# A four-stage sequence model on one core: the scan's output sum split over three engines, its start rewritten, and the last two stages reordered

## The reference

```
x = _layernorm(x + _L0_attn_ref(x, ...))   # state-space scan, 64 heads of 8, state 64
x = _layernorm(x + _L0_ffn_ref(x, ...))    # 8 experts, top 2, plus a shared expert
x = _layernorm(x + _L1_attn_ref(x, ...))   # A = sum over tokens of cos_sim(K) * V;  Y = (A * rope(Q)) @ W_out
x = _layernorm(x + _L1_ffn_ref(x, ...))    # silu(x Wg) * (x Wu) @ Wd, integer weights with scales
```

```
h = a_t * h + u_t * b_t          # b_t and c_t are rotated by phi
y = einsum('bhpn,bhn->bhp', h, c_t)
```

## Time and profile before

| | |
|---|---|
| median of 3 runs | 2555.78 us (2555.35 to 2564.16) |
| the profiled execution's own time | 2558.58 us |
| its span, first to last instruction | 2556.9 us |
| mean granted TensorE clock, share of full speed | 0.928 |
| busy over the span | DVE 1908.7 us (75%), PE 2052.8 (80%), ACT 1529.7 (60%), POOL 1479.2 (58%) |
| the scan, first DVE product to last y | 202.6 to 1414.0 us |
| key-value stage | about 2044 to 2262 us |
| last stage | about 2266 to 2557 us |

### The profile page before, as it was taken

How to read it: one execution, slowest core, us unless ns; L and a number is a source line. 1 busy time by engine, 2 the same in 40 slices (tenths; PEclk the granted TensorE clock), 3 DMA queues, 4 the chain that set the end, 5 groups by cost and what they waited for, 6 DMA issues and landing times. The chain is left out here.

```text
span 2556.9 us, 60194 instructions
## 1 busy us (share of the span) xinstructions
PE 2052.8 (80%) x19761; PEld 1532.8 (60%) x19761; DVE 1908.7 (75%) x4991; ACT 1529.7 (60%) x2922; POOL 1479.2 (58%) x2287
## 2 busy tenths in 40 slices
PE   8955778878878888877887799686799857768887
PEld 5634555655556556555555688564455445558887
DVE  4547999999999999999999344466333267757776
ACT  5648999999999999999995122354122112222222
POOL 2447888888888888888887132343111154425454
PEclk9977999999999999999997899887899978989998
DMA  5766766676676776767664477343222244311110
GB/s 168 244 199 176 182 180 184 175 191 172 173 188 174 178 190 174 185 179 182 181 177 115 139 231 220 121 143 111 83 85 85 63 127 126 123 55 38 49 49 29
DMA packets 295156, 373.66 MB, mean 146 GB/s; under 512 B 44628, under 2 KB 234646, under 8 KB 294902
## 3 DMA queue, kind: packets, MB, share of 16 engines
q1 hardware_dynamic: 285030, 343.10, 48.5%
q0 software_dynamic: 9872, 27.28, 3.3%
HBM read 151.03 MB, written 85.00 MB: 92 GB/s over the span
## 5 line engine op out<-in xcount | busy, mean ns | idle before, releaser
L668 POOL TENSOR_TENSOR p_CR<-p_pc 128x256 f32<-128x256 f32 x512 | 373.8, 730 | 132.5 <-DVE p_pc L993 113.6
L749 PE MATMUL p_ps_sc<-p_CR,p_BR 64*128 64x128 f32 x4096 | 316.3, 296 | 159.4 <-DVE p_M L1010 115.5
L749 PEld LDWEIGHTS p_ps_sc<-p_CR,p_BR 64*128 64x128 f32 x4096 | 270.2, 198 | 216.9 <-issue 170.3
L672 POOL TENSOR_TENSOR p_BR<-p_pb 128x256 f32<-128x256 f32 x512 | 373.6, 730 | 36.6 <-DVE p_pb L1002 13.4
L883 ACT ACTIVATE p_D<-p_ps_x 128x512 f32<-128x512 f32 x512 | 289.7, 593 | 85.9 <-PE p_ps_x L715 84.7
L1010 DVE TENSOR_TENSOR p_M<-p_ps_sc,p_D 128x1024 f32<-128x1024 f32 x256 | 310.4, 1212 | 6.0 <-issue 3.2
L993 DVE SCALAR_TENSOR_TENSOR p_pc<-p_ps_c,p_beta,p_cs 128x256 f32<-128x256 f32 x512 | 242.9, 474 | 32.2 <-DMA p_sn<-p_tr_s 28.7
L764 PE MATMUL p_ps_y<-p_M,p_uexp 128*32 128x128 f32 x4096 | 254.0, 278 | 0.0
L1002 DVE SCALAR_TENSOR_TENSOR p_pb<-p_ps_b,p_beta,p_sn 128x256 f32<-128x256 f32 x512 | 242.6, 474 | 0.0
L1002 DVE SCALAR_TENSOR_TENSOR p_pb<-p_ps_b,p_beta,p_cs 128x256 f32<-128x256 f32 x512 | 242.5, 474 | 0.0
L993 DVE SCALAR_TENSOR_TENSOR p_pc<-p_ps_c,p_beta,p_sn 128x256 f32<-128x256 f32 x512 | 242.5, 474 | 0.0
(11 more groups left out here) (279 smaller groups left out, 5191.4 us busy)
## 6 DMA issues: line engine op xcount, KB each, us to landing
p_cs<-p_tr_c SPq DMA_DIRECT2D x256, 256.0 KB
p_sn<-p_tr_s SPq DMA_DIRECT2D x256, 256.0 KB
p_phib<-scratch_phi SPq DMA_DIRECT2D x256, 128.0 KB
p_x<-scratch_rt SPq DMA_DIRECT2D x72, 128.0 KB, 2.0
scratch_ro<-p_o POOLq DMA_DIRECT2D x72, 128.0 KB, 2.0
p_xT<-in_xT SPq DMA_DIRECT2D x64, 128.0 KB, 4.5
scratch_u<-p_u SPq DMA_DIRECT2D x16, 512.0 KB, 3.5
scratch_wu<-p_wu SPq DMA_DIRECT2D x16, 512.0 KB, 4.3
```

What stands on the lines that cost most here:

```text
L668: e.tensor_tensor(CR[:, p, g, :], pc[:, g % 2, 0, :], pc[:, g % 2, 1, :], ALU.add).then_inc(S["rotC"], 1)
L672: e.tensor_tensor(BR[:, p, g, :], pb[:, g % 2, 0, :], pb[:, g % 2, 1, :], ALU.add).then_inc(S["rotB"], 1)
L749: m = e.matmul(sc_ps[half][:, (g * 2 + b) * L:(g * 2 + b + 1) * L], BR[half * 64:half * 64 + 64, p, 2 * q + g, b * L:(b + 1) * L], CR[half ...
```

## The change

**Scan, body.** DVE's two instructions of `outputs` become one: it only scales the state's part, into the second half of a tile y of twice the size. ACT copies the chunk's part from PSUM into the first half (`sums_out`, after decays 4 and 5 of the next step). POOL adds the halves at the end of the step (`outputs`, after its last pair of rotations). ACT's second rounding pass now takes two parts u at once, 128x512 instead of twice 128x256, after every second u; so POOL's `turns` waits for a pair of parts.

**Scan, start.** The frequencies and the first angles are loaded ahead of the constants; ACT runs one Sin at once (tile warm); the sine half of the first spreading is issued by ACT's own queue; POOL no longer does `turns(2, 0, 0)` ahead of the first step; ACT's work for steps 2 and 3 is woven into step 0 (`first_step`).

**Key-value stage.** Of the four gathers of a step on POOL two move to the step's start and two stay between the two norms.

**Last stage.** `project` moves from the step's middle to the end of the step before; `turn` moves ahead of up part 2; `attention` is cut in two (sums and statistics ahead of gated part 0, the output `residual` behind it), and so is the last norm; `high_x` moves ahead of gated part 2; POOL's and ACT's streams follow.

The core of the diff in the scan (POOL's turns and its new `outputs`, ACT's new `sums_out` and its rounding, DVE's `outputs`):

```diff
             def turns(s, p, u):
...
-                at_least(e, S["mg_ok"], s, 3 * NQ, 3 * u + 3)
+                at_least(e, S["mg_ok"], s, TURNS, 5 * (u // 2) + 5)
...
+            def outputs(t, p):
+                at_least(e, S["y_ev"], t, 1, 1)
+                at_least(e, S["yx_ok"], t, 1, 1)
+                e.tensor_tensor(y[:, p, 0, :], y[:, p, 0, :], y[:, p, 1, :], ALU.add).then_inc(S["y_ok"], 1)
...
+            def sums_out(t, p):
+
+                at_least(e, S["yi_mm"], t, U, U)
+                at_least(e, S["yx_mm"], t, U, U)
+                if t >= 2:
+                    at_least(e, y_out[p], t - p, 8, 0)
+                at_least(e, S["yx_ok"], t, 1, 1)
+                e.activation(y[:, p, 0, :], yi_ps, ACT.Copy).then_inc(S["y_ev"], 1)
...
-                at_least(e, S["mg_ok"], s, 3 * NQ, 3 * u + 2)
-                e.activation(mg[:, u, :], mg[:, u, :], ACT.Copy, bias=-MAGIC).then_inc(S["mg_ok"], 1)
+                if u % 2:
+                    at_least(e, S["mg_ok"], s, TURNS, 5 * (u // 2) + 4)
+                    e.activation(mg[:, u - 1:u + 1, :], mg[:, u - 1:u + 1, :], ACT.Copy, bias=-MAGIC).then_inc(S["mg_ok"], 1)
...
-                e.tensor_tensor(yx[:, p, :], yx_ps, et[:, p, :], ALU.mult).then_inc(S["yx_ok"], 1)
-                at_least(e, S["yx_ok"], t, 1, 1)
...
-                e.tensor_tensor(y[:, p, :], yi_ps, yx[:, p, :], ALU.add).then_inc(S["y_ok"], 1)
+                e.tensor_tensor(y[:, p, 1, :], yx_ps, et[:, p, :], ALU.mult).then_inc(S["yx_ok"], 1)
```

and in the last stage, PE's step (TensorE's order; `left` counts the steps that follow):

```diff
                 up(t, p, 0)
                 if later:
                     down(t - 1, 2)
-                if not last:
-                    project(t + 1, 1 - p)
                 up(t, p, 1)
                 if later:
                     down(t - 1, 3)
+                if left:
+                    turn(t + 1, 1 - p)
                 up(t, p, 2)
-                if not last:
-                    turn(t + 1, 1 - p)
                 up(t, p, 3)
                 down(t, 0)
                 down(t, 1)
+                if left == 2:
+                    project(t + 2, p)
```

More of the change, by code:

```diff
@@ L673, in step @@
                     if g % 2:
-                        if g < NG - 1 and t + 2 < T:
+                        if t == 0:
+                            for u in ((), (0, 1), (2, 3), ())[g // 2]:
+                                turns(2, 0, u)
+                        elif g < NG - 1 and t + 2 < T:
                             turns(t + 2, p, g // 2 + 1)
@@ L679, in step @@
                             stage_u(t, p, g // 2, b)
+                    if g == 7 and t:
+                        outputs(t - 1, 1 - p)
             for s in range(2):
@@ L838, in _ @@
         def _(e):
-            e.wait_ge(S["zeroed"], 5)
-            e.wait_ge(S["const_in"], 112)
+            e.wait_ge(S["zeroed"], 1)
+            e.activation(warm[:, :], quart[:, :], ACT.Sin).then_inc(S["warm"], 1)
+            e.wait_ge(S["freq_in"], 16)
             def signed_bc(c):
@@ L946, in state, with first_step @@
                                  ).then_inc(S["x_ok" if h else "kept"], 1)
+            def first_step():
+                for n in range(2, U):
+                    decays(0, n)
+                    s, u = (2, n - 2) if n < 6 else (3, n - 6)
+                    in_turns(s, s, u)
+                    whole_turns(s, s, u)
+                turned(0, 0)
+                magnitude(2, 0)
+                for n in range(2):
+                    decays(1, n)
+                in_turns(3, 3, 2)
+                whole_turns(3, 3, 2)
+                sines(2, 0)
+                turned(0, 1)
+                in_turns(3, 3, 3)
+                whole_turns(3, 3, 3)
             def all_turns(s):
@@ L2093, in step @@
             def step(t, p):
+                if t + 2 < NC:
+                    gather(t + 2, p, 0)
                 if t:
@@ L2102, in _ @@
             for t in range(2):
-                gather(t, t)
+                for b in range(BATCH):
+                    gather(t, t, b)
             norm_pool(e, S2, N2, 0, mhalf)
@@ L2444, in down, with step @@
                 m.then_inc(S["o_mm"], 1)
-            def step(t, p, last=False):
+            def step(t, p, left=2):
                 later = not (isinstance(t, int) and t == 0)
@@ L2492, in step @@
                                      scale=gs[:, 2 * n + i:2 * n + i + 1]).then_inc(S["silu_ok"], 1)
-                    if n == 2 and not last:
+                    if n == 1 and not last:
                         copy_turned(t + 1)
@@ L2564, in sums, with last_out @@
                 e.tensor_tensor(xs[:, :, :], xm[:, :, :], xk[:, p, :, :], ALU.add).then_inc(S["xs_ok"], 1)
[L2566 to L2572 removed]
+            def last_out(t, p):
+                if not (isinstance(t, int) and t < 2):
+                    at_least(e, S["stored"][p], t - p, 8, 0)
+                norm_out(e, S2, N2, t, xs, x4[:, p, :, :])
             def step(t, p, last=False):
                 later = not (isinstance(t, int) and t == 0)
+                if not last:
+                    attention(t + 1, 1 - p)
                 gated(t, 0)
                 if not last:
[L2578 removed]
+                    residual(t + 1, 1 - p)
                 gated(t, 1)
@@ L2581, in step @@
                     sums(t - 1, 1 - p)
-                gated(t, 2)
                 if not last:
                     high_x(t + 1, 1 - p)
+                gated(t, 2)
+                if later:
+                    at_least(e, S["xs_ok"], t - 1, 1, 1)
+                    norm_stats(e, S2, N2, t - 1, xs)
                 gated(t, 3)
                 if later:
-                    last_norm(t - 1, 1 - p)
+                    last_out(t - 1, 1 - p)
             attention(0, 0)
+            residual(0, 0)
             high_x(0, 0)
```

112 lines of the change are left out of this document (61 added, 51 removed).

## The result

The changed kernel takes 2494.87 us (median of 4 runs, 2490.43 to 2499.15) against 2558.83 (4 runs, 2555.35 to 2564.16): a ratio of 0.9748, 95% interval 0.9721 to 0.9775. It is faster, but by 64 us where 98 were forecast, and lies above the forecast's range (to 2472) and above the range for 8 in 10 (to 2490). The profiled execution took 2490.43 with a span of 2488.8, 68.1 less than before.

| stretch | forecast | measured | from |
|---|---|---|---|
| scan, start to the first y product | -8.5 | -2.7 | 237.1 to 234.4 |
| scan, body | -28.4 + 3 | -15.0 | 63 steps of 18.67, now of 18.43 |
| scan, tail | +0.4 | +0.8 | last product's start to last y's end, 0.9 to 1.75 |
| key-value stage | -25 | -26.5 | first sums to PE's first Y, 216.9 to 190.4 |
| last stage | -40 + 1 | -25.0 | first Y to the end, 286.45 to 261.4 |

What follows compares the result with a forecast made beforehand. It took DVE to bound the scan and PE the last stage. Terms -8.5 - 28.4 + 0.4 + 3 - 25 - 40 + 1 = -97.5 took the profiled 2558.58 to 2461.1, median 2458 us, range 2444 to 2472.

Steps and rivals of the forecast that it cites:

- Last stage, -40: Last stage: 15 steps fall from 16.8 to 14.1 us, saving 40 us, with bounds 25 (15.1 a step) and 46.
- DVE only 0.1 below: Last stage: a walk with old durations had PE bound the step at 13.65 us, DVE finishing just under that.
- DVE bounds the last stage: Rival, last stage: waits and register instructions make DVE's step 15.1 us or more, not 14.1; about 2475 us; chance 0.08.
- The rival of the loop's jump: Last stage: jumps back, six times a pass, show on PE, costing up to 24 us, about 2475 us; chance 0.15.
- POOL's add blocks DVE: Rival, scan: each POOL add of 0.73 us holds DVE up, so 46 us come back, 2504 us; chance 0.05.
- Scan, body, -28.4: Scan body: DVE's pair of instructions becomes one, saving 0.45 us in each of 63 steps, if DVE stays the bound.
- +3 for the waits: Scan body: DVE's 7 us of waiting for the spread sines grows by 3 us, bounds 0 and 7.
- covered: Scan body: ACT's 17.5 to 17.7 us fits the new 18.22 us step; otherwise each 0.1 us more costs 6 us.
- the scan keeps its step: Rival, scan: ACT or the ring of its copies and PE's exponents needs 18.6 us; 28 us stay, 2486 us; chance 0.08.
- Scan, start, -8.5: Scan start: earlier angles and Sin table save 4.6 us, an earlier first M 4.0; together 8.5, bounds 4.6 and 11.
- the second part comes back as a later wait: Scan start: bound case where the 4.0 us from the earlier first M is lost again, leaving 4.6 us saved.
- Key-value stage, -25: Key-value stage: two fewer gathers ahead of POOL's root cut DVE's waits, saving 25 us, bounds 15 and 28.

Runs made afterwards that it cites:

- Experiment 2: Changed kernel with DVE's norm outputs in the last stage moved ahead of the roundings that start POOL's subtractions: 2464.55 us, ratio to before 0.9621.
- experiment 3: Changed kernel, order untouched, with POOL's low-part subtractions in the last stage's loop cut to 32 of 512 columns: 2467.52 us, ratio to before 0.9604.
- Experiment 4: Changed kernel with SyncE's six loads of B and C split, three in each of two scan steps: 2480.16 us, ratio to before 0.9673.
- experiments 5 and 6: Kernel before with the scan's output sum alone split over DVE, ACT and POOL: 2583.86 us; the second adds the wide rounding pass: 2547.51 us.
- experiments 8 and 9: Changed kernel with ScalarE's turns ahead of its exponentials in the first scan step: 2490.04 us; changed kernel with SyncE issuing the first sine spreading: 2489.54 us.
- experiment 11: Changed kernel with norm outputs and sum xs ahead of the roundings, B and C loads in halves, ScalarE's turns first: 2450.56 us, ratio to before 0.9538.

## Why the prediction was wrong where it was

**Last stage, -40 with "DVE only 0.1 below" PE.** The step that failed is "DVE, each piece as long as in the step of the earlier trace rows, where they make 12.33". Its pieces are not of one length wherever they stand. Before the change the norm outputs ran behind a wait for POOL's root, and so while POOL had nothing else; the new order hides that wait by putting them behind the rounding that releases POOL's subtraction. Experiment 2 moved them out, experiment 3 shortened POOL's work, and both brought 0.41 to 0.45 us and PE-bound steps back. The rival "DVE bounds the last stage" (0.08) named the right bound and nearly the right step (15.1 or more; 15.5 measured), but its cause, waits and register instructions, was wrong: it needed 2.8 us of idle on DVE a step, and there are 15.54 - 14.70 = 0.84. That the stage gained just the 25 of the forecast's near bound is luck: the bound was set for that other cause. The rival of the loop's jump is refuted by experiment 2, in which PE runs through the jumps without a gap.

The same prediction set a rule on this very port beside the rival "POOL's add blocks DVE", and there it held: DVE's products, with one input in PSUM, are still 0.47 us beside POOL's adds. I asked of the engine that *gained* work, and not of the instructions whose *neighbours* changed. The Trainium skill (SBUF — State Buffer, Who interferes with whom) has a tensor_scalar between SBUF tensors contend with GpSimd when it can run in a mode that uses both of VectorE's ports, and has the one that comes second blocked for the whole instruction of the first. The trace agrees: 0.41 us free, 1.39 at the most beside a subtraction of 1.3 to 1.4. By the same rule xs, with two SBUF inputs, should be blocked too, and it is: 1.23 against 0.69.

**Scan, body, -28.4 "if DVE stays the bound", +3 for the waits.** The saving on DVE was right, the term for the waits mis-sized: 13 us where I took 3 and bounded it by 7. I had scaled the waits with the step. They are not a share of the step, but what is left over when SyncE's issuing comes late in the step behind the loads of B and C, and a shorter step leaves SyncE less time. Experiment 4 shows it for 10 us of waits. That ScalarE's work is "covered" was right for the pair of edits and only just: without the wide pass, 0.45 us more a step on ScalarE cost 0.49 us a step (experiments 5 and 6); "each 0.1 us more on ACT would cost 6 us" makes 27 us of the one, and 31 came out. The lower clock of experiment 5 is in those 31, so the price of ScalarE's work alone is not shown. It is the ring that the rival "the scan keeps its step" named, and it closed where the wide pass was missing.

**Scan, start, -8.5.** ScalarE's first turn came 4.2 us sooner (3.3 forecast), its cosine 5.1 (4.6) and the first product 3.1. The earlier first M was nearly as forecast (-7.0), and "the second part comes back as a later wait", there a bound, is what happened: POOL waits for ScalarE's pass with the rotations behind it. The two queues were taken for no loss or a gain; they were a loss of 1.3 us, with ScalarE held for 5.9. Neither, mended alone, brought the kernel's end forward by as much as 1 us (experiments 8 and 9); in experiment 11, with the loads split, the earlier start was kept. That SyncE's lateness is what swallowed it before is argued from the waits for the sines, which grew by 3.1 us in experiment 8, and was not tested by itself. The Trainium skill (DMA: Bandwidth & Descriptors, Issuing engines are not separate DMA queues) has the transfers of all issuing engines run on the same DMA engines and interleave; the trace agrees, with 6.8 and 7.3 us from issue to landing beside each other and 4.2 and 4.4 from one queue. An issue took 1.44 to 1.48 us on each queue beside the other and 0.86 to 0.99 alone.

**Key-value stage, -25**: right in cause and size (-26.5). The waits ahead of the second norm's output are 0.24 to 0.25 us but for the first, 0.81; in the last step of the stage before it was 0.21.

## What to carry to other kernels

When an order changes, look at each moved instruction's new neighbour on the engines that share something with it, not only at its inputs: a hidden wait can turn into a longer instruction, and then a walk made of old durations says that an engine just fits when it doesn't. Where the trace shows small waits on a queue at every fourth step, count that queue's issue time in that step before taking anything off the step. And two edits that look apart can be one: the split sum was a gain of 13 us of scan beside the wide pass and a loss of 17 without it.

## What the runs showed of the hardware that was not expected

- A norm output of 128x256 between SBUF tensors takes 0.41 us, and up to 1.39 beside POOL's subtraction of 128x512; a sum of two SBUF tensors of 128x512 takes 0.69 and 1.23. Products with an input in PSUM stay at 0.47.
- Four transfers of 256 KB take 3.2 to 4.4 us to issue on one queue; on SyncE's and ScalarE's queue at once they take 5.91 and 5.75 and land later (6.8 and 7.3 us after their issue, against 4.2 and 4.4), and the engine whose queue it is does nothing else meanwhile.
- PE ran 170 us without a gap through the jumps of a loop.
